# Gated cross-attention and a top-2 expert layer: the two projections of a step cut in half around its scores, and the row maxima split into two bf16 parts before their transposition

## The reference

```python
x = x + tanh(g_xattn) * attention(layernorm(x), ctx, ctx)   # rope on q and k, 16 heads of 8, biases
x = x + tanh(g_ffn) * ffn(layernorm(x))

# attention: softmax(Q K^T / sqrt(8)) V for each head, then @ Wo^T + bo
# ffn: xn = rms_norm(x) * scale; scores = xn @ w_router^T (8 experts); top 2; c = softmax(scores) at them
#      out = x + sum over the two experts of c * (val * silu(gate)) @ w_down, [val, gate] = xn @ w_up
```

## Time and profile before

| | us |
|---|---|
| median of 3 runs | 436.27 |
| lowest and highest run | 434.77, 436.6 |
| the profiled execution, as timed | 435.61 |
| its span, first to last instruction | 433.8 |
| TensorE busy | 391.3 |
| VectorE busy | 302.5 |
| ScalarE busy | 260.1 |

### The profile page before, as it was taken

One profiled execution on the slowest core, in us unless ns is written; L12 is line 12 of the kernel. 1 busy time (PEld: TensorE's weight loads), 2 busy tenths in 40 slices (PEclk: granted clock), 3 DMA queues, 4 the chain that ended last, 5 costly groups with the idle time before them and its releaser, 6 DMA issues.

```text
span 433.8 us, 13431 instructions
## 1 busy us (share of the span) xinstructions
PE 391.3 (90%) x3876; PEld 267.6 (62%) x3877; DVE 302.5 (70%) x1167; ACT 260.1 (60%) x582; POOL 244.8 (56%) x201
## 2 busy tenths in 40 slices
PE   8997888999889888988998899998999999999991
PEld 3445454565656545555655578686777878778771
DVE  5878878898898978979786565568655555555550
ACT  3518577786967768676756665644455555454540
POOL 7073233135665555745343367888887458876663
PEclk9999999999999999999998999999999999999997
DMA  7525152353867914325101324544454334444320
GB/s 198 157 60 137 28 133 67 88 145 108 223 162 206 217 55 111 102 58 132 52 29 47 98 59 78 92 65 98 78 76 59 50 48 57 62 52 57 34 24 0
DMA packets 57423, 39.08 MB, mean 90 GB/s; under 512 B 8819, under 2 KB 55158, under 8 KB 57366
## 3 DMA queue, kind: packets, MB, share of 16 engines
q1 hardware_dynamic: 43622, 28.87, 26.1%
q0 software_dynamic: 12736, 8.64, 14.2%
q10 hardware_dynamic: 1008, 0.85, 0.8%
HBM read 14.26 MB, written 11.75 MB: 60 GB/s over the span
## 4 chain that ended last, share of the span: by engine, by line
PE 50%; DVE 17%; DMA 11%; issue 7%; SPq 6%; ACT 4%; POOLq 2%; POOL 1%; DVEq 0%; ACTq 0%
PE bank L1614 9%; PE bank L1592 7%; PE bank L1594 7%; DMA out<-ys,yi 5%; DVE nmx L847 5%; DMA ks<-parts 4%; PE bank L1604 4%; SPq L249 4%; PE bank L1374 3%; PE bank L1401 2%; PE bank L1348 2%; SPq L282 2%; PE bank L1316 2%; PE bank L1317 2%; ACT pt L580 2%
## 5 line engine op out<-in xcount | busy, mean ns | idle before, releaser
L516 POOL DMA_INDIRECT out<-ys,yi x72 | 111.8, 1553 | 43.5 <-issue 23.0
L427 POOL DMA_INDIRECT slots_dram<-xr,slu x64 | 65.5, 1024 | 75.0 <-ACT onT L593 55.1
L847 DVE TENSOR_REDUCE nmx<-bank 128x4 f32<-128x512 f32 x128 | 81.7, 680 | 4.3 <-PE bank L1348 4.3
L580 ACT ACTIVATE pt<-bank 128x512 f32<-128x512 f32 x128 | 72.5, 595 | 9.3 <-PE bank L1361 8.2
L1614 PEld LDWEIGHTS bank<-wf_sb,hT 128*128 128x128 f32 (+1 forms) x432 | 56.9, 190 | 22.7 <-issue 18.0
L1200 DVE TENSOR_TENSOR hh<-sg,bank 128x352 f32<-128x352 f32 x72 | 37.4, 520 | 47.9 <-ACT sg L714 27.2
L1614 PE MATMUL bank<-wf_sb,hT 128*128 (+1 forms) x432 | 61.0, 277 | 4.7 <-DVE hT L1210 4.6
L722 ACT ACTIVATE ys<-bank,yc 128x128 f32<-128x128 f32 x72 | 26.5, 368 | 64.0 <-PE bank L1614 60.1
L1592 PE MATMUL bank<-wf_sb,xT 128*128 x144 | 55.2, 465 | 0.1
L1594 PE MATMUL bank<-wf_sb,xT 128*128 x144 | 54.3, 459 | 0.0
L1374 PE MATMUL bank<-pt,v 128*9 128x128 f32 x1024 | 49.4, 276 | 3.7 <-ACT pt L580 2.5
(11 more groups left out here) (193 smaller groups left out, 707.9 us busy)
## 6 DMA issues: line engine op xcount, KB each, us to landing
qs<-parts SPq DMA_DIRECT2D x48, 128.0 KB
ks<-parts SPq DMA_DIRECT2D x45, 128.0 KB
xs<-slots_dram SPq DMA_DIRECT2D x72, 66.0 KB
wf_sb<-in_wup SPq DMA_DIRECT2D x8, 352.0 KB
x_sb<-in_x SPq DMA_DIRECT2D x8, 256.0 KB, 3.7
ctx_sb<-in_ctx_in SPq DMA_DIRECT2D x8, 256.0 KB, 4.5
out<-x_sb SPq DMA_DIRECT2D x8, 256.0 KB, 2.5
out<-ys,yi POOLq DMA_INDIRECT x72, 3.4
```

Source lines behind the costliest of these rows:

```text
L427: nc.gpsimd.indirect_dma_start(out=slots_dram, out_offset=bass.IndirectOffsetOnAxis(ap=slu[:, c % 2, k, kk:kk + 1], axis=0), in_=xr[:, c % ...
L516: nc.gpsimd.indirect_dma_start(out=out.rearrange("b s d -> (b s) d"), out_offset=bass.IndirectOffsetOnAxis(ap=yi[:, r:r + 1], axis=0), in_ ...
L580: nc.scalar.activation(pt[:, 4 * g:4 * g + 4, :], STB[g % 2][:, :].rearrange("p (h s) -> p h s", h=4), ACT.Exp, scale=SCORE_SCALE).then_in ...
L847: nc.vector.tensor_reduce(nmx[:, b % 2, at:at + 4], SB[g % 2][:, :].rearrange("p (h s) -> p h s", h=4), AX.X, ALU.max, negate=True).then_i ...
```

## The change

- **Maxima.** VectorE now splits the maxima before they are transposed: `split_high` copies nmx (128 x 16) to bf16, `split_low` subtracts, both from SBUF to SBUF, into a new tile nm2. TensorE transposes both parts at once, as one bf16 matmul with 32 columns of nm2 as weights against a bf16 identity, where it had one float32 transposition. ScalarE copies the 32 rows to mTs (`maximum_out`), ahead of the next `heads_out`. SyncE and the next scores wait for this copy.
- **Projections.** Each is cut into a cosine and a sine half. The cosine half stays where it was, and the sine half goes behind the third group of scores (queries) or behind the transposition of the attended rows (keys). In these steps all four groups of weighted values move back behind them.
- **ScalarE.** In the steps with a projection the high part is taken after the exponentials 2 and 3. `maximum_out` stands at the end of each step, but at u = 3 ahead of `middle` and `base`.
- **VectorE.** The remainder moves behind the maxima 2 and 3. At u = 3 the addition of the attention and its statistics come first, then the remainder.
- **GpSimd.** The low part of the queries also waits for the split, that of the keys for the masks of the experts.
- The transposed rows go to bank 6 and no longer to bank 7 (but for chunk 6), and the next heads wait for their copy. `project_out` comes ahead of `transpose_maximum` in every step.

```diff
-                nc.vector.tensor_copy(mTs[:, b % 2, 0, :], mT_ps).then_inc(d_mh, 1)
+                nc.vector.tensor_copy(nm2[:, b % 2, 0, :], nmx[:, b % 2, :]).then_inc(d_mh, 1)
...
-                nc.vector.tensor_tensor(mTs[:, b % 2, 1, :], mT_ps, mTs[:, b % 2, 0, :], ALU.subtract).then_inc(d_mT, 1)
+                nc.vector.tensor_tensor(nm2[:, b % 2, 1, :], nmx[:, b % 2, :], nm2[:, b % 2, 0, :], ALU.subtract).then_inc(d_ms, 1)
...
             def transpose_maximum(b):
-                pe.wait_ge(d_max, 4 * b + 4)
-                nc.tensor.transpose(mT_ps, nmx[:, b % 2, :], ident).then_inc(pe_mT, 1)
+                pe.wait_ge(d_ms, b + 1)
+                mm(mT_ps, nm2[:, b % 2, :, :].rearrange("p a h -> p (a h)"), identb, start=True, stop=True).then_inc(pe_mT, 1)
...
+            def maximum_out(b):
+                act.wait_ge(pe_mT, b + 1)
+                if b >= 2:
+                    act.wait_ge(m_in[b % 2], 32 * (b // 2))
+                nc.scalar.activation(mTs[:, b % 2, :], mT_ps, ACT.Copy).then_inc(a_mT, 1)
...
+                        if there(c - 2):
+                            pool.wait_ge(d_mb, c - 1)
                         low(c + 1, 1)
...
+                        pool.wait_ge(d_ms, b + 3)
                         low(c + 2, 0)
...
+                if projects and u == 3:
+                    maximum_out(b + 2)
                 if u == 3 and there(c + 2):
                     middle(c + 2, 0)
                 if u == 3 and there(c - 1):
                     base(c - 1)
+                if real(b + 2) and not (projects and u == 3):
+                    maximum_out(b + 2)
```

146 lines of the change are left out of this document (89 added, 57 removed).

## The result

The changed kernel takes 449.5 us (four runs, 447.15 to 452.22) against 436.0 us of the kernel before, measured beside it (434.77 to 436.6). The ratio is 1.033, with a 95% interval of 1.029 to 1.037: 13.5 us slower, where 7 were forecast. The profiled execution of after took 447.15 us, its span is 445.4 us and its mean granted clock of TensorE 0.972 (before: 433.8 us and 0.991). The other three had clocks of 0.958 to 0.968. Three more comparisons on other chips gave 1.029, 1.033 and 1.031. Every ratio here is one of fast runs: executions over 1.5% above the fastest of the same kernel are left out of it, two of the kernel before with 493.65 and 1978.15 us among them.

A forecast was written before the change was run, and what follows sets the result against it. A chunk's loop over several engines, with ScalarE nearly continuous before the maxima, was taken as the bound. 435.61 us + 10.2 (stalls) - 0.35 - 2.2 (last steps), about 0.3 off for transpositions: 443.0 us, range 434 to 449 us.

The forecast's parts named there:

- A stall at the split of u = 3, passed on by ScalarE: TensorE idles 1.3 us for VectorE's late split; ScalarE starts middle and base 1.86 us later; 440 to 447 us, chance 0.62.
- The term of a chunk: Maxima sent 1.8 us later in each of chunks 1 to 5, 1.2 us in chunk 0: together +10.2 us.
- The wait for the heads in u = 0: TensorE's wait for the heads in chunks 1 to 5 becomes about 1.3 us and not 0.63.
- The stretch from the maxima to the next first scores: From SyncE sending the maxima, through the stacks, to the next chunk's scores: fixed at 6.47 us while transfers come last.
- The gain in the last steps: Steps 24 to 29, without stalling projections, each 0.37 us shorter as VectorE or the loop through its division sets pace: 2.2 us.
- the cheaper transpositions: One cheaper matmul per transposition, 0.05 us; about 0.3 us off in all where TensorE is the last to come.
- VectorE freed: Rival: VectorE sets the pace and gains about 0.45 us a step, u = 1 excepted: 421 or 428 us; chance 0.20.
- Slower still: Rival: split held by GpSimd or costing as much as what it replaces, u = 2 stalling 0.5 us: 450 us; chance 0.10.

The follow-up runs named there:

- e5: Changed kernel with VectorE splitting directly behind the fourth maximum in u = 3 and ScalarE doing middle and base ahead of maximum_out: 1.000 of before, 436.0 us.
- e15: Changed kernel with TensorE's idle times filled by matmuls of no use, shorter than the waits: 1.030 of before, the changed kernel beside it 1.031.
- e2: Changed kernel with only ScalarE's order altered in u = 3, middle and base ahead of maximum_out, the split left in place: 1.018 of before.
- e12: e5 plus matmuls of no use at the start, count_rows at the end of step 26, and maxima transposed and copied earlier in u = 0: 0.998 of before.

## Why the prediction was right and where it was wrong

- **Direction and mechanism: right.** A stall at the split of u = 3, passed on by ScalarE. TensorE idles 0.99 us (forecast 1.3), its transposition starts 13.59 us behind the chunk's first scores (13.45), `base` starts 1.97 us later (1.86). In u = 2 TensorE waits 0.68 us (0.9). Undoing both orders takes the whole loss away (`e5`).
- **The term of a chunk: about right, with luck in it.** 1.8 us per chunk were forecast, 1.3 to 2.35 us are measured at full clock. The wait for the heads in u = 0 is 1.39 us in chunk 5 (forecast 1.3); in chunk 2, where the clock holds TensorE itself back, 0.44 us. The stretch from the maxima to the next first scores, taken as fixed at 6.47 us, is 5.8 to 7.1 us.
- **No stretch at 1.2 GHz was in the sum: this failed.** I worked with durations at full clock and let TensorE wait for free. In chunk 0 the step behind the split takes 9.10 us at a clock of 0.81; in another execution, on another chip, with the same wait of 1.98 us ahead of it and the clock full, it takes 8.05. Chunk 3 begins with a step of 8.46 us for 7.36. Chunk 2 takes 30.27 us, 1.4 us more than chunk 1; 0.55 of these are a longer wait for the stacks and the rest the clock. Together some 3 us in the trace of after.
- **Why the sum to step 24 was off by less.** By the marks, step 24 comes 11.5 us later than before; forecast were 9.85. The start gave 1.3 us back that I had put at 0. Chunks 0 to 4 are 2.4, 2.35, 3.3, 1.25 and 1.3 us longer (forecast: 1.2, then 1.8 each), and up to step 24 2.2 us more follow. Chunk 3 looks cheap because in before it takes 28.4 us, with waits for the maxima and the stacks of its own. So errors of both signs met.
- **The gain in the last steps: failed.** I took 2.2 us, and 0.3 us for the cheaper transpositions, off. Steps 24 to the last gained nothing: the shift is 11.5 us at step 24 and 11.7 at the last heads. Steps 24 to 28 take 5.10, 5.89, 6.69, 5.91 and 5.84 us, for 5.01, 6.24, 5.61, 5.88 and 5.84 before. One step gains 0.35 us, as forecast for all six, and step 26 loses 1.1 by its wait of 1.04 us. Of `count_rows` the diff showed a new wait, and I had not costed it. In step 27 of after TensorE is busy for all of the 5.91 us, so it sets the pace there, and not VectorE.
- **The size of the miss.** The forecast was 443.0 us and 449.5 were measured, just outside the range of 434 to 449 us. The 6.5 us are 1.65 up to step 24, 2.5 for the gain that did not come, and 2.35 between the profiled execution, 447.15 us, and the median of the four, of which the other three had a lower clock.
- **The rival "VectorE freed": fell.** VectorE idles 35.2 us for the scores ahead of its maxima in after, and 4.3 in before. **"Slower still"** gave the right time, 450 us, by luck, for a wrong reason: splits take 0.14 to 0.22 us, as assumed, and u = 2 is not longer.

How much of the loss is the clock's stays open. Among executions of the changed kernel on one chip the time rises by about 0.24 us with each microsecond at 1.2 GHz (15 executions in four comparisons; 0.2 to 0.5 for most other kernels). In the three later comparisons the changed kernel has 17 to 25 us more at 1.2 GHz than before. By that, an estimate from these numbers, some 4 to 6 of the 13.5 us go with it. But in `e15` the clock was raised by as much and the time stayed, since the waits for the stacks grew. Shown are 1.3 us per stretch in one step of `e2`, 3.7 us at the start (`e15`), 0.7 us per chunk in `e12`, and that without the two orders there is no loss.

## What to carry to other kernels

When an operation moves behind others on one engine, look for who waits for it on a second engine and what stands behind it in order on a third; here each of the two orders alone left a loss of 1 to 2%, and only both undone together left none. Where TensorE is at full clock, a forecast should count a new idle time twice: once as a wait, and as a possibility once more, as matmuls at half speed behind it, which cost only where TensorE is the bound. And each wait in the diff is to be costed, also one far from the change's center: one cost 1.1 us in step 26, and two others, on GpSimd, saved 12.5 us in the kernel that has the maxima's part alone.
